# Gated feed-forward: the rounding of x with the grid offset made by a maximum inside VectorE's sums, and the subtraction moved to VectorE

## The chip, the cores and the metric

The kernel runs on one core of a Trainium2 chip. The metric is the device time of one execution in microseconds (us); of several runs the median is taken. The engines are named as in the profile: PE is TensorE (PEld its weight loads), DVE is VectorE, ACT is ScalarE, POOL is GpSimd, SP is SyncE.

## The reference

Six sub-blocks work on x, of shape (2, 2048, 256): twice a feed-forward with two routed experts and a shared one around a linear attention, then twice a gated feed-forward around a softmax attention. The change touches only the gated feed-forward, `_L1_ffn_ref`. Each of its three matrix products rounds both operands to a 4-bit grid with one scale for each block of 16 values:

```python
def fp4_quant_dequant(x):
    xb = x.reshape(shape[:-1] + (shape[-1] // BLOCK, BLOCK))      # BLOCK = 16
    scale = jnp.max(jnp.abs(xb), axis=-1, keepdims=True) / 6.0
    scale = jnp.maximum(scale, jnp.float32(1e-12))
    xn = xb / scale
    idx = jnp.searchsorted(_MID, jnp.abs(xn))
    q = _GRID[idx] * jnp.sign(xn) * scale        # 0, 0.5, 1, 1.5, 2, 3, 4, 6
    return q.reshape(shape)
...
gate = fp4_linear(x, w_gate)                     # 256 -> 704
y = fp4_linear(x, w_up)                          # 256 -> 704
h = jax.nn.silu(gate) * y
return fp4_linear(h, w_down)                     # 704 -> 256
...
x = x + 0.5 * _L1_ffn_ref(_layernorm(x, axis=-1), L1_ffn_w_gate, L1_ffn_w_up, L1_ffn_w_down)
```

## The kernel before

`build_program` writes six stages one after the other: `ffn0("a")`, `attn0()`, `ffn0("b")`, `ffn1("a", False)`, `attn1()`, `ffn1("b", True)`. The two calls of `ffn1` are the gated feed-forward, called the first and the second pass here. The order on each engine is written by hand, and every wait is on a semaphore.

The 4096 rows of x are 32 tiles of 128 rows (`T` = 32), which stay in SBUF. The weights were rounded to the grid in an earlier stage. A tile t goes through `ffn1` like this. ScalarE normalises it (L1684, tile `fxn`). The rounding of x, called x below (tiles `fxb`, `fxy`, `fxq`; 256 columns), runs three tiles ahead of the products (`AHEAD` = 3). TensorE transposes the rounded tile (L1591), ScalarE copies it out as a high part (L1691), TensorE subtracts that in PSUM (L1598), and ScalarE copies the rest, the low part (L1695). TensorE makes the gate and the up product from both parts (L1606, L1611). ScalarE applies Silu to the gate (L1718), VectorE multiplies by the up product in PSUM (L1774, tile `fh`, 704 columns). The rounding of h (tiles `fqb`, `fqy`, `fhq`; 704 columns) is done in the next turn of the loop. Three turns after its products (`LAG` = 3) TensorE transposes h (L1620, L1627, L1628), ScalarE copies its high part (L1723) and low part (L1732), and TensorE makes the down product (L1636 from the high part, L1642 from the low part, which waits for L1732). VectorE adds it to x (L1742), and in the first pass it also makes the statistics of the row for the next stage (L120, L122). The second pass (`store`) writes x out instead.

The rounding, class `QuantiseFour`, is the same for x and h. With s the scale of a block and y = v/s, adding c = max(1.5, |y|) x `STEP` to y rounds y in the float's last bits, and subtracting c again leaves the grid value. The steps are:

- step 0, L155: the largest absolute value of each block of 16, on VectorE; steps 1 and 2, L157 and L159: s and 1/s, on VectorE, on 16 columns for x and 44 for h
- step 3, L193: y, on VectorE; then |y| on ScalarE, L205
- step 4, L197: c = max(|y|, 1.5) x `STEP`, on VectorE, with one input tensor
- step 5, L201: r = y + c, on VectorE
- L175: r - c on GpSimd; L177: times s, on GpSimd

`order(t)` alternates the six steps of x of tile t + 3 with the six of h of tile t - 1 on VectorE; L1774 stands behind the eighth of the twelve, that is between step 3 and step 4. At the head of each turn stands L1742 of tile t - 4. In each turn GpSimd does L175 and L177 of h and then L175 and L177 of x. Before the loop VectorE rounds the x of tiles 0, 1 and 2 without anything between them, and GpSimd does their two operations, and between these it makes the low parts of the three weight matrices (L1798).

Of the kernel before, what the change touches and what calls it, by code (L numbers as in the profile page):

```python
# [11 lines left out]
ALU = mybir.AluOpType  # L12
ACT = mybir.ActivationFunctionType
AX = mybir.AxisListType

P = 128
# [6 lines left out]
BELOW = 1.0 - 2.0 ** -24  # L23
EXPONENT = 0x7F800000
MAGIC = 1.5 * 2.0 ** 22
STEP = 2.0 ** 22 - 4.0


class Event:
# [28 lines left out]
def build_program(nc, A):  # L58
    x_in = A["L0_attn_x"]
    nb, L, D = x_in.shape  # L60
# [19 lines left out]
    with ExitStack() as ctx:  # L80
        known = {}

        def event(name, by=1):
            if name not in known:
                known[name] = Event(ctx.enter_context(nc.semaphore(name)), by)
            return known[name]

        def sb(name, shape, dt=F32, scope=ctx):
            return scope.enter_context(nc.sbuf_tensor(name, shape, dt))

        def ring(scope, name, shape, n, dt=F32):
            return [sb(f"{name}{i}", shape, dt, scope) for i in range(n)]
# [17 lines left out]
        dv = Chain(ctx.enter_context(nc.semaphore("vector_own")))  # L110
# [24 lines left out]
        def blocks(ap):  # L135
            return ap.rearrange("p (k j) -> p k j", j=QB)

        class Quantise:
# [12 lines left out]
            def vector(self, e, step):  # L151
                if step > 0:
                    e.wait_ge(*self.at)
                if step == 0:
                    made = e.tensor_reduce(self.amax, blocks(self.src), AX.X, ALU.max, apply_absolute_value=True)  # L155
                if step == 1:
                    made = e.tensor_scalar(self.s, self.amax, INV_MAX, SCALE_FLOOR, ALU.mult, ALU.max)  # L157
                if step == 2:
                    made = e.reciprocal(self.rs, self.s)  # L159
                if step == 3:  # L160
                    made = e.scalar_tensor_tensor(out=blocks(self.y), in0=blocks(self.src), scalar=BELOW,
                                                  in1=self.spread(self.rs), op0=ALU.mult, op1=ALU.mult)
                if step == 4:
                    made = e.tensor_scalar(self.c.bitcast(I32), self.y.bitcast(I32), EXPONENT, None,
                                           ALU.bitwise_and)
                if step == 5:
                    made = e.tensor_scalar(self.c, self.c, 1.0, MAGIC, ALU.max, ALU.mult)
                if step == 6:
                    e.tensor_tensor(self.r, self.y, self.c, ALU.add).then_inc(*self.summed.up)
                    return  # L170
                made.then_inc(*dv.up())
                self.at = dv.now()

            def gpsimd(self, e):
                e.tensor_tensor(self.r, self.r, self.c, ALU.subtract).then_inc(*pl.up())  # L175
                e.wait_ge(*pl.now())
                e.tensor_tensor(blocks(self.out), blocks(self.r), self.spread(self.s),  # L177
                                ALU.mult).then_inc(*self.done.up)

        class QuantiseFour(Quantise):  # L180
# [3 lines left out]
            def events(self, n, scaled, magnitude):  # L184
                self.number, self.scaled, self.magnitude = n, scaled, magnitude
                return self

            def vector(self, e, step):
# [6 lines left out]
                if step == 4:  # L195
                    e.wait_ge(*self.magnitude(self.number + 1))
                    e.tensor_scalar(self.c, self.c, 1.5, STEP, ALU.max, ALU.mult).then_inc(*dv.up())  # L197
                    self.at = dv.now()
# [4 lines left out]
            def scalar(self, e):  # L203
                e.wait_ge(*self.scaled(self.number + 1))
                e.activation(self.c, self.y, ACT.Abs).then_inc(*self.magnitude.up)  # L205

        def constants():
            with nc.Block() as block:

                @block.vector  # L210
                def _(e):
                    e.memset(eps[:], LN_EPS).then_inc(*eps_ok.up)

                @block.gpsimd
                def _(e):
                    e.memset(wdT[R1:P, C1 - 1, :], 0.0).then_inc(*pl.up())
                    e.wait_ge(*pl.now())
                    e.memset(ident[:], 0.0).then_inc(*pl.up())
                    e.wait_ge(*pl.now())
                    e.affine_select(out=ident[:], in_=ident[:], compare_op=ALU.not_equal, fill=1.0, base=0,  # L220
                                    pattern=[[-1, P]], channel_multiplier=1).then_inc(*ident_ok.up)

                @block.sync
                def _(e):
                    e.dma_start(x[:, 0:GT, :], xin[:, 0:GT, :]).then_inc(*x_in_ok[0].up)

                @block.tensor
                def _(e):
                    e.wait_ge(*ident_ok(1))

                @block.scalar
                def _(e):
                    e.wait_ge(*eps_ok(1))
# [1304 lines left out]
        def ffn1(tag, store):  # L1538
            with ExitStack() as scope:
                W1 = C1 * P  # L1540
                XN, XQ = ring(scope, f"fxn{tag}", [P, D], 2), ring(scope, f"fxq{tag}", [P, D], 4)
# [5 lines left out]
                TMX = [(sb(f"fxb{tag}{i}", [P, 3, D // QB], scope=scope), sb(f"fxy{tag}{i}", [P, 3, D], scope=scope))  # L1547
                       for i in range(2)]
# [10 lines left out]
                xn_ok, xsum, xq_ok, xturn, xhi = (event(f"f1_{n}") for n in ("xn", "xsum", "xq", "xturn", "xhi"))  # L1559
# [4 lines left out]
                xy, xabs, hy, habs = (event(f"f1_{n}") for n in ("xy", "xabs", "hy", "habs"))  # L1564
# [3 lines left out]
                    return ap.rearrange("p (j n) -> p j n", j=2)  # L1568

                def quantise_x(t):  # L1570
                    return QuantiseFour(XN[t % 2][:], D, P, TMX[t % 2], XQ[t % 4][:], xsum, xq_ok).events(t, xy, xabs)

                def quantise_h(t):
                    return QuantiseFour(HB[t % 2][:], H1, P, TMH[t % 2], HQ[t % 3][:, 0:H1], hsum, hq_ok).events(t, hy, habs)
# [7 lines left out]
                with nc.Block() as block:  # L1582
# [97 lines left out]
                    def _(e):  # L1680
# [20 lines left out]
                        normal(0)  # L1701
                        normal(1)
                        quantise_x(0).scalar(e)
                        normal(2)
                        quantise_x(1).scalar(e)
                        e.activation(wu[0][:], wuT[:], ACT.Copy).then_inc(*whi_ok.up)
                        normal(3)
                        quantise_x(2).scalar(e)
                        e.activation(wd[0][:], wdT[:], ACT.Copy).then_inc(*whi_ok.up)
                        high_x(0)  # L1710
# [561 lines left out]
```

## Time and profile before

| what | value |
|---|---|
| median of 3 runs | 3412.04 us (3410.95 to 3433.1) |
| the profiled execution | 3422.33 us, its span 3420.3 us |
| busy over the span | PE 3212.1 us (94%), DVE 2529.7 (74%), ACT 2023.8 (59%), POOL 736.3 (22%) |
| first pass, about 1205 to 1500 us | PE 256.22 of 295, DVE 261.73, ACT 151.37, POOL 157.65 |
| second pass, about 3146 to 3420 us | PE 246.36 of 274, DVE 241.86, ACT 148.83, POOL 172.87 |

The profile is of one execution, which took 10 us more than the median, so a step is costed against its own span, and the difference is then set against the median. A timeline row gives the start from the span's beginning and the duration, both in us, then engine, line, operation, output<-inputs and shapes; in brackets stands the idle time of the engine before it and what ended that. An operation that had to wait for a port after it was started shows the wait in its duration and not in brackets. Numbers of double buffers are left out of names, and the last letter of a name, a or b, is the pass.

### The profile page before, as it was taken

Reading aid. Unit: us, or ns where it says so; the run is one execution under the profiler, and the core shown is the slowest. Engines: PE = TensorE matmul, PEld = TensorE weight load, DVE = VectorE, ACT = ScalarE, POOL = GpSimd, SP = SyncE. Lnnn points to the kernel's source line nnn. Section 1 sums busy time; section 2 is a strip of 40 time slices with the busy share of each in tenths; the row PEclk is TensorE's granted clock in tenths of the full one; section 3 lists DMA queues with packets and bytes.
Section 4 is the critical chain, followed back from the end, with each engine's and each line's share of the span. In section 5 each row is a group of like instructions: output and inputs, shape, how many; then the busy total and the mean of one; then the engine's idle time right before and its main releaser. Section 6 shows DMA issues by size and latency. Waiting matters only on the chain. (4 is left out here: it accounts for less than half of the span.)

```text
span 3420.3 us, 54248 instructions
## 1 busy us (share of the span) xinstructions
PE 3212.1 (94%) x20420; PEld 2117.2 (62%) x20420; DVE 2529.7 (74%) x4826; ACT 2023.8 (59%) x3764; POOL 736.3 (22%) x740
## 2 busy tenths in 40 slices
PE   7999979997999979988999999999999999997999
PEld 6899967776899969963444333344333333332998
DVE  7433658766433689948888888998888999972997
ACT  5544534335544545542777777777677777765554
POOL 3322334443322355520000000000000000001665
PEclk9999989999999989996999989999989999987999
DMA  3210210002211200023003030302003030000000
GB/s 127 79 44 32 62 45 1 1 2 78 73 44 38 62 1 1 1 76 49 14 26 50 2 39 2 39 1 31 9 2 38 2 39 2 2 2 0 13 14 25
DMA packets 60930, 99.91 MB, mean 29 GB/s; under 512 B 7632, under 2 KB 44160, under 8 KB 57984
## 3 DMA queue, kind: packets, MB, share of 16 engines
q1 hardware_dynamic: 54144, 78.62, 10.5%
q0 software_dynamic: 6528, 17.83, 1.6%
q8 instruction: 164, 2.69, 0.3%
q14 instruction: 94, 0.77, 0.1%
HBM read 65.36 MB, written 30.93 MB: 28 GB/s over the span
## 5 line engine op out<-in xcount | busy, mean ns | idle before, releaser
L2186 DVE TENSOR_REDUCE smxp<-psum 128x1 f32<-128x512 f32 x2048 | 1277.3, 683 | 159.0 <-PE psum L2051 144.9
L2146 ACT ACTIVATE spr<-psum 128x512 f32<-128x512 f32 x2048 | 1082.5, 599 | 453.6 <-PE psum L2070 445.5
L2070 PE MATMUL psum<-sqs,sks 50*128 50x512 f32 x2048 | 754.7, 470 | 5.4 <-ACT spr L2146 2.8
L2051 PE MATMUL psum<-sks,sqs 48*128 48x512 f32 x2048 | 678.4, 458 | 13.2 <-DMA sqs<-q_parts 12.8
L2051 PEld LDWEIGHTS psum<-sks,sqs 48*128 48x128 f32 x2048 | 292.7, 199 | 523.3 <-issue 462.0
L2084 PE MATMUL psum<-spr,sv 128*32 128x512 f32 x4096 | 576.9, 636 | 1.8 <-ACT spr L2146 0.7
L2070 PEld LDWEIGHTS psum<-sqs,sks 50*128 50x128 f32 x2048 | 323.3, 194 | 199.0 <-ACT spr L2146 167.9
L1801 POOL MEMSET fhqb<- 128x64 f32 x3 | 0.3, 152 | 1651.5 <-POOLq L1964 1651.5
L490 PE MATMUL psum<-w_a,hsa_hi 128*128 128x256 f32 (+1 forms) x1088 | 198.4, 281 | 0.1
L490 PE MATMUL psum<-w_b,hsb_hi 128*128 128x256 f32 (+1 forms) x1088 | 197.2, 280 | 0.4 <-DVE hsb_lo L740 0.4
L490 PEld LDWEIGHTS psum<-w_a,hsa_hi 128*128 128x128 f32 x1088 | 176.2, 189 | 12.6 <-DVE hsa_lo L740 1.2
L740 DVE TENSOR_TENSOR hsb_lo<-hidb,hsb_hi 128x512 fp32r<-128x512 f32 x136 | 94.3, 694 | 120.9 <-ACT hidb L585 120.3
L490 PEld LDWEIGHTS psum<-w_b,hsb_hi 128*128 128x128 f32 x1088 | 175.4, 188 | 12.3 <-DVE hsb_lo L740 0.9
L740 DVE TENSOR_TENSOR hsa_lo<-hida,hsa_hi 128x512 fp32r<-128x512 f32 x136 | 95.5, 703 | 116.4 <-ACT hida L585 115.7
L2084 PEld LDWEIGHTS psum<-spr,sv 128*32 128x32 f32 x4096 | 83.0, 110 | 152.3 <-issue 125.2
L490 PE MATMUL psum<-w_a,hsa_lo 128*128 128x256 f32 (+1 forms) x544 | 152.4, 280 | 0.0
L490 PE MATMUL psum<-w_b,hsb_lo 128*128 128x256 f32 (+1 forms) x544 | 151.9, 279 | 0.0
L473 PE MATMUL psum<-xTa_hi,w_a 128*128 128x512 f32 x288 | 106.8, 413 | 4.9 <-DVE xTa_lo L729 3.5
L473 PE MATMUL psum<-xTb_hi,w_b 128*128 128x512 f32 x288 | 104.9, 406 | 3.3 <-DVE xTb_lo L729 1.9
L490 PEld LDWEIGHTS psum<-w_a,hsa_lo 128*128 128x128 f32 x544 | 102.9, 189 | 0.0
L490 PEld LDWEIGHTS psum<-w_b,hsb_lo 128*128 128x128 f32 x544 | 102.4, 188 | 0.0
L584 ACT ACTIVATE hsa_hi<-psum,bwa 128x512 fp32r<-128x512 f32 x64 | 44.1, 689 | 97.4 <-issue 83.6
(417 smaller groups left out, 6149.8 us busy)
## 6 DMA issues: line engine op xcount, KB each, us to landing
sks<-q_parts SPq DMA_DIRECT2D x42, 256.0 KB, 9.4
sqs<-q_parts SPq DMA_DIRECT2D x42, 256.0 KB, 19.8
q_parts<-spart SPq DMA_DIRECT2D x16, 512.0 KB, 3.0
f_routed_a<-yoa SPq DMA_DIRECT2D x9, 512.0 KB, 2.9
f_routed_b<-yob SPq DMA_DIRECT2D x9, 512.0 KB, 2.9
x<-in_L_attn_x_dram SPq DMA_DIRECT2D x8, 512.0 KB, 7.3
yoa<-in_L_ffn_w_dram SPq DMA_DIRECT2D x16, 256.0 KB, 2.6
xga<-f_sorted_a SPq DMA_DIRECT2D x8, 512.0 KB, 3.8
```

The lines of the kernel that those rows point to most:

```text
L473: m = e.matmul(psum[:, n % 3, :], w[u][:, k, :], XT[p % 2][v][:, k, :], start=(k == j == 0), stop=(k == KD - 1 and j == 2))
L490: m = e.matmul(ops[:, i // 2, (i % 2) * D:(i % 2 + 1) * D], hs[u][:, i * P:(i + 1) * P], w2[:, v, ex, c, :], start=(c == 0 and i % 2 == 0 ...
L584: e.activation(hi[:], psum[:, n % 3, :], ACT.Relu, bias=bias)
L740: e.tensor_tensor(lo[:], HB[n % 2][:], hi[:].bitcast(F32), ALU.subtract).then_inc(*low_ok.up)
L1801: m = e.memset(hq[:, H1:], 0.0)
L2051: e.matmul(bank(what), QS[n % 2][rows, pr, q0:q0 + P], KS[n % 2][rows, pr, jc * GW:(jc + 1) * GW], start=True, stop=True, tile_position=(H ...
L2070: e.matmul(st[s % 3], KS[n % 2][rows, pr, jt * P:(jt + 1) * P], QS[n % 2][rows, pr, ic * GW:(ic + 1) * GW], start=True, stop=True, tile_po ...
L2084: m = e.matmul(po[32 * hq:32 * hq + VW, :], VB[b][:, jt, c0:c0 + VW], PR[j % 2][:, hq, :], start=(jt == 0), stop=(jt == TB - 1), tile_posi ...
L2146: e.activation(PR[j % 2][:, hq, :], st[s % 3], ACT.Exp, scale=float(DH) ** -0.5).then_inc(*exp_ok.up)
L2186: e.tensor_reduce(out[:, r // (2 * GT * IC), r // (2 * IC) % GT, r // 2 % IC, r % 2:r % 2 + 1], bank(what), AX.X, ALU.max).then_inc(*pm_fr ...
```

## The change

For x, class `QuantiseFour` is replaced by a new class, `QuantiseMax`; h stays as it was. Step 3 makes -y; ScalarE makes |y| x `STEP` through the scale of the activation. Step 4 takes the maximum with `LEAST` = 1.5 x `STEP`, which is c, and adds -y to it in one instruction, so that c is never written. Step 5 makes the same maximum again and subtracts what step 4 left from it, which gives the rounded y. GpSimd only multiplies by s.

```diff
+LEAST = 1.5 * STEP
...
+        class QuantiseMax(Quantise):
...
+            def vector(self, e, step):
+                if step < 3:
+                    super().vector(e, step)
+                if step == 3:
+                    e.wait_ge(*self.at)
+                    e.scalar_tensor_tensor(out=blocks(self.y), in0=blocks(self.src), scalar=-BELOW,
+                                           in1=self.spread(self.rs), op0=ALU.mult, op1=ALU.mult).then_inc(*self.scaled.up)
+                if step == 4:
+                    e.wait_ge(*self.magnitude(self.number + 1))
+                    e.scalar_tensor_tensor(out=self.r, in0=self.c, scalar=LEAST, in1=self.y, op0=ALU.max,
+                                           op1=ALU.add).then_inc(*dv.up())
+                    self.at = dv.now()
+                if step == 5:
+                    e.wait_ge(*self.at)
+                    e.scalar_tensor_tensor(out=self.r, in0=self.c, scalar=LEAST, in1=self.r, op0=ALU.max,
+                                           op1=ALU.subtract).then_inc(*self.summed.up)
+
+            def scalar(self, e):
+                e.wait_ge(*self.scaled(self.number + 1))
+                e.activation(self.c, self.y, ACT.Abs, scale=STEP).then_inc(*self.magnitude.up)
+
+            def gpsimd(self, e):
+                e.tensor_tensor(blocks(self.out), blocks(self.r), self.spread(self.s),
+                                ALU.mult).then_inc(*self.done.up)
...
                 def quantise_x(t):
-                    return QuantiseFour(XN[t % 2][:], D, P, TMX[t % 2], XQ[t % 4][:], xsum, xq_ok).events(t, xy, xabs)
+                    return QuantiseMax(XN[t % 2][:], D, P, TMX[t % 2], XQ[t % 4][:], xsum, xq_ok).events(t, xy, xabs)
```

The two places at which the prediction looks are these. On VectorE (DVE), from step 3 of x in one turn of the loop in the first pass (tiles of x: `fxya`, of h: `fqya`), before and then after:

```order
L193 SCALAR_TENSOR_TENSOR fxya<-fxna,fxba 128x256
L193 SCALAR_TENSOR_TENSOR fqya<-fha,fqba 128x704
L1774 TENSOR_TENSOR fha<-psum,fsga 128x704
L197 TENSOR_SCALAR fxya<-fxya 128x256
L197 TENSOR_SCALAR fqya<-fqya 128x704
L201 TENSOR_TENSOR fxya<-fxya 128x256
L201 TENSOR_TENSOR fqya<-fqya 128x704
L1742 SCALAR_TENSOR_TENSOR x<-psum,x 128x256
```

```order
L223 SCALAR_TENSOR_TENSOR fxya<-fxna,fxba 128x256
L194 SCALAR_TENSOR_TENSOR fqya<-fha,fqba 128x704
L1810 TENSOR_TENSOR fha<-psum,fsga 128x704
L227 SCALAR_TENSOR_TENSOR fxya<-fxya 128x256
L198 TENSOR_SCALAR fqya<-fqya 128x704
L232 SCALAR_TENSOR_TENSOR fxya<-fxya 128x256
L202 TENSOR_TENSOR fqya<-fqya 128x704
L1778 SCALAR_TENSOR_TENSOR x<-psum,x 128x256
```

Nothing moves there; two instructions of x have another form (L227 for L197, L232 for L201), and the line numbers are higher. On GpSimd (POOL), the start of the second pass up to the first rounding of h (`fqyb`, `fhqb`), before and then after:

```order
L1798 TENSOR_TENSOR fwg_lob<-wgT,fwg_hib 128x1408
L175 TENSOR_TENSOR fxyb<-fxyb 128x256
L177 TENSOR_TENSOR fxqb<-fxyb,fxbb 128x256
L175 TENSOR_TENSOR fxyb<-fxyb 128x256
L177 TENSOR_TENSOR fxqb<-fxyb,fxbb 128x256
L1798 TENSOR_TENSOR fwu_lob<-wuT,fwu_hib 128x1408
L175 TENSOR_TENSOR fxyb<-fxyb 128x256
L177 TENSOR_TENSOR fxqb<-fxyb,fxbb 128x256
L1798 TENSOR_TENSOR fwd_lob<-wdT,fwd_hib 128x1536
L175 TENSOR_TENSOR fxyb<-fxyb 128x256
L177 TENSOR_TENSOR fxqb<-fxyb,fxbb 128x256
L175 TENSOR_TENSOR fqyb<-fqyb 128x704
```

```order
L1834 TENSOR_TENSOR fwg_lob<-wgT,fwg_hib 128x1408
L240 TENSOR_TENSOR fxqb<-fxyb,fxbb 128x256 x2
L1834 TENSOR_TENSOR fwu_lob<-wuT,fwu_hib 128x1408
L240 TENSOR_TENSOR fxqb<-fxyb,fxbb 128x256
L1834 TENSOR_TENSOR fwd_lob<-wdT,fwd_hib 128x1536
L240 TENSOR_TENSOR fxqb<-fxyb,fxbb 128x256
L176 TENSOR_TENSOR fqyb<-fqyb 128x704
L178 TENSOR_TENSOR fhqb<-fqyb,fqbb 128x704
```

The subtractions of x (L175 on `fxyb`) are gone there, 32 in each pass, and the multiplies (L240, before L177) follow one another or the work on h.

## Rows read from the trace of the kernel before

**Rows 1.** Windows view, busy us per engine (x instructions), clock: steady stretches of both passes.

```profile
1262.00:1479.00 217.00, 208.55 (x1437) 199.05 (x1437) 204.89 (x418) 116.52 (x208) 121.59 (x106) 1.00 0.00 1
...
3193.00:3405.00 212.00, 211.07 (x1498) 205.25 (x1497) 200.88 (x379) 120.22 (x216) 143.34 (x110) 1.00 0.06 19
```

**Rows 2.** DVE timeline, L1742 at either end of 25 tiles, then one.

```profile
1254.07 0.42 DVE L1742 SCALAR_TENSOR_TENSOR x<-psum,x 128x256 f32<-128x256 f32 x1
...
1455.68 0.42 DVE L1742 SCALAR_TENSOR_TENSOR x<-psum,x 128x256 f32<-128x256 f32 x1 [0.29 <-PE psum L1642]
...
3192.78 0.43 DVE L1742 SCALAR_TENSOR_TENSOR x<-psum,x 128x256 f32<-128x256 f32 x1
...
3380.38 0.42 DVE L1742 SCALAR_TENSOR_TENSOR x<-psum,x 128x256 f32<-128x256 f32 x1 [0.28 <-PE psum L1642]
...
3387.68 0.42 DVE L1742 SCALAR_TENSOR_TENSOR x<-psum,x 128x256 f32<-128x256 f32 x1 [0.17 <-PE psum L1642]
```

**Rows 3.** DVE timeline, one tile of the first pass (start us, us).

```profile
1353.03 0.86 DVE L157 TENSOR_SCALAR fxba<-fxba 128x16 f32<-128x16 f32 x1
...
1354.39 0.48 DVE L193 SCALAR_TENSOR_TENSOR fxya<-fxna,fxba 128x256 f32<-128x256 f32 x1
1354.79 1.30 DVE L193 SCALAR_TENSOR_TENSOR fqya<-fha,fqba 128x704 f32<-128x704 f32 x1
...
1357.79 0.88 DVE L201 TENSOR_TENSOR fqya<-fqya 128x704 f32<-128x704 f32 x1
```

**Rows 4.** POOL timeline, the same tile of the first pass.

```profile
1352.48 1.39 POOL L177 TENSOR_TENSOR fhqa<-fqya,fqba 128x704 f32<-128x704 f32 x1
1353.83 0.76 POOL L175 TENSOR_TENSOR fxya<-fxya 128x256 f32<-128x256 f32 x1
1354.66 0.68 POOL L177 TENSOR_TENSOR fxqa<-fxya,fxba 128x256 f32<-128x256 f32 x1
```

**Rows 5.** PE timeline, the same tile: idle time before it in brackets.

```profile
1357.94 0.98 PE L1642 MATMUL psum<-fwd_hia,fhTa_lo 128*128 128x256 f32 x6 [0.31 <-ACT fhTa_lo L1732]
```

**Rows 6.** DVE timeline, one tile of the second pass.

```profile
3267.88 0.42 DVE L1742 SCALAR_TENSOR_TENSOR x<-psum,x 128x256 f32<-128x256 f32 x1 [0.27 <-PE psum L1642]
...
3269.34 0.17 DVE L157 TENSOR_SCALAR fxbb<-fxbb 128x16 f32<-128x16 f32 x1
...
3270.03 1.15 DVE L193 SCALAR_TENSOR_TENSOR fxyb<-fxnb,fxbb 128x256 f32<-128x256 f32 x1
3271.10 1.42 DVE L193 SCALAR_TENSOR_TENSOR fqyb<-fhb,fqbb 128x704 f32<-128x704 f32 x1
```

**Rows 7.** POOL timeline, the same tile of the second pass.

```profile
3267.69 1.72 POOL L175 TENSOR_TENSOR fqyb<-fqyb 128x704 f32<-128x704 f32 x1 [2.17 <-DVE fqyb L201]
3269.48 1.42 POOL L177 TENSOR_TENSOR fhqb<-fqyb,fqbb 128x704 f32<-128x704 f32 x1
3270.86 0.92 POOL L175 TENSOR_TENSOR fxyb<-fxyb 128x256 f32<-128x256 f32 x1
3271.86 1.15 POOL L177 TENSOR_TENSOR fxqb<-fxyb,fxbb 128x256 f32<-128x256 f32 x1
```

**Rows 8.** Source views, durations ns min/median/max: DVE forms of 256 columns.

```profile
L193 DVE SCALAR_TENSOR_TENSOR fxya<-fxna,fxba x32: 363/480/1223, 1214.8 to 1451.1; 128x256 f32<-128x256 f32 x32
...
L197 DVE TENSOR_SCALAR fxya<-fxya x32: 276/278/2726, 1215.7 to 1453.5; 128x256 f32<-128x256 f32 x32
...
L201 DVE TENSOR_TENSOR fxya<-fxya x32: 409/414/426, 1216.0 to 1454.2; 128x256 f32<-128x256 f32 x32
...
L789 DVE SCALAR_TENSOR_TENSOR x<-yoa,x x32: 403/418/426, 382.6 to 426.5; 128x256 f32<-128x256 f32 x32
```

**Rows 9.** DVE timeline, second x tile before the first pass's loop.

```profile
1216.84 0.47 DVE L157 TENSOR_SCALAR fxba<-fxba 128x16 f32<-128x16 f32 x1
...
1217.63 0.63 DVE L193 SCALAR_TENSOR_TENSOR fxya<-fxna,fxba 128x256 f32<-128x256 f32 x1
```

**Rows 10.** POOL timeline, the same stretch.

```profile
1217.36 0.62 POOL L177 TENSOR_TENSOR fxqa<-fxya,fxba 128x256 f32<-128x256 f32 x1
```

More of the change, by code:

```diff
@@ L205, in scalar, with events @@
                 e.activation(self.c, self.y, ACT.Abs).then_inc(*self.magnitude.up)
+        class QuantiseMax(Quantise):
+            def events(self, n, scaled, magnitude):
+                self.number, self.scaled, self.magnitude = n, scaled, magnitude
+                return self
+            def vector(self, e, step):
[20 more added lines that the diff above has]
+                                ALU.mult).then_inc(*self.done.up)
         def constants():
```

## The prediction

> **What bounds the kernel now.** I read the busy time by stage first, since the change touches only the two gated feed-forward passes (the fourth and the last of the six stages). In their steady stretches TensorE is busy 96% and over 99% of the time and VectorE 94% and 95% [rows 1], so the shares don't say which of them sets the pace. The spacing of the residual add L1742, one per tile, does better: from 1254.07 to 1455.68 there are 25 tiles, 8.06 us each, in the first pass, and from 3192.78 to 3380.38 again 25, 7.50 each, in the second [rows 2]. The tile after that, without an x to quantise, takes 7.30 us with TensorE at work throughout. So some 7.3 us is what TensorE needs, and there are 0.8 us a tile above it in the first pass, 0.2 in the second.
>
> I call the instructions by line, with x or h for what they quantise: L177h is GpSimd's multiply of h. The timelines of VectorE and GpSimd laid side by side show where the 0.8 us go. L157x is an operation on 16 columns and takes 0.86 us: it ends at 1353.89, when L177h on GpSimd has just ended (1353.87). L193x ends at 1354.87, 0.28 after L175x (1354.59); L193h ends at 1356.09, 0.75 after L177x (1355.34) [rows 3, 4]. The second pass shows the same and the reverse: L193x ends 0.28 after L177h; L175x, which started at 3270.86, ends 0.60 after L193x; L193h ends 0.74 after L175x; and L177x, which takes 0.62 alone [rows 10], ends 0.49 after L193h, having taken 1.15 [rows 6, 7]. The two engines take turns: GpSimd's operations exclude VectorE's two-input ones (256 columns cost 0.27 of such time, 704 columns 0.74) and the other way round. I call what they take turns at the port. The reduction and the product from PSUM at L1774 aren't held.
>
> **The loop that sets the period** is then one through both engines. In the first pass, with T the end of L177h (1353.87): L193h ends at T+2.22, L201h at T+4.80 (1358.67), and the next L177h at T+8.06. Nothing in it waits except for the port. The other loop, L193h to ScalarE to TensorE's L1642 to L1742 and back, has slack: L1642 starts 1.85 after L193h ends, waiting 0.31 for ScalarE, and is done at 1358.92 [rows 5], 2.83 after it; L1742 and what follows reach L157x some 0.84 us before the port is free. In the second pass no statistics follow L1742, VectorE asks for the port earlier in GpSimd's cycle, L157x slips through between L175h and L177h, and it is L193x that waits (1.15 us) until L177h is done.
>
> **The change, part by part.** *Form of the scaling and of Abs:* a sign and a factor, same shapes, nothing. *First sum:* a tensor_scalar of 256 columns, 0.278, becomes a scalar_tensor_tensor with two inputs. The same form in place elsewhere, L789, takes 0.418; the difference is +0.14 [rows 8]. *Subtraction:* the tensor_tensor of 0.414 becomes a scalar_tensor_tensor of 0.418, +0.00 [rows 8]. Both lie behind L1774, when GpSimd has finished with the tile's work, so no port wait is added; but they are on the loop, between L193h and L201h, so the 0.14 counts in full. *GpSimd:* the subtraction L175x goes, and the multiply L177x follows L177h at once.
>
> First pass: L157x ends at T+0.02 as before, L193x starts at T+0.52. The multiply starts at T-0.04 and takes 0.62 [rows 10], a little more for the hold by VectorE's small operations, so it is over at T+0.58 to T+0.62. L193x alone takes 0.36 [rows 8], of which the last 0.27 need the port: it would take it at T+0.61, and hardly waits. It ends at T+0.88, not T+1.00; L193h starts 0.08 before that and takes 0.88, as L201h does [rows 3], with nothing to wait for: T+1.68, not T+2.22. That is -0.54 for the waits and +0.14 for the sum, **-0.40 a tile**, 7.66 us. Covers: TensorE needs 7.3, so L1774, which waits for the tile's second product, finds it ready at this pace; L1742 could start 0.15 after L201h instead of 0.29, and L157x would still come 0.98 before T. So the same loop stays the bound, and 25 tiles give -10.0 us.
>
> Second pass: L193x still waits for L177h and ends 0.28 after it. Then the multiply (0.49 of port time) stands where the subtraction did (0.60), and L193h waits for it, -0.11 or -0.10. With +0.14 the tile gets longer by 0.03, 7.53 us; 25 tiles give +0.8, and the three without L1742 at the start of each pass, which show this second pattern too, +0.2. The bounds of a tile here are +0.14, if the multiply holds the port as long as the subtraction, and -0.2, where TensorE's 7.3 stops any gain.
>
> Before the loop, in both passes, tiles 0 to 2 are quantised one after the other, and L157x (0.47) and L193x (0.63, ending 0.28 after L177x) are held by GpSimd for tiles 1 and 2 [rows 9, 10]. Without the subtraction I put them at 0.35 and 0.42, -0.33 a tile, against +0.14 each for tiles 0 and 1: -0.4 us until ScalarE may write the first transposed x, which TensorE waits for. Bounds: 0 and -0.9, the length of one subtraction with its handover. Twice -0.4 is -0.8.
>
> **Sum:** -10.0 + 0.8 + 0.2 - 0.8 = -9.8 us. The profiled execution took 3422.3 us (span 3420.3) and would take 3412.5; the median of the timed runs lies 10 us lower, at 3412.0, and as no row ties that difference to the feed-forward, I take the same -9.8 off it: **3402 us**.
>
> **A page against a row.** The row: one two-input operation and one GpSimd operation never overlap in their port time [rows 6, 7]. The Trainium skill, SBUF — State Buffer, on the shared port pair, has it as an exclusive lock, held for a whole instruction, taken by whoever starts first; the trace agrees on the exclusion. If both engines shared the port's rate instead, the relief would be half as large, some -5 us. The Trainium skill, Perfetto Trace Analysis, Optimizing Scalar/DVE Operations, says for the same reason that moving operations between GpSimd and VectorE "might not help"; and that a saturated VectorE may give work away, which is the reverse of this change.
>
> **Rivals.** *The multiply takes the subtraction's place in the first pass too, slower (0.17).* The place is L193x at T+0.6. If the multiply isn't quite over there and L193x goes first, the multiply resumes behind it, and L193h waits again: T+2.12, -0.10 + 0.14 = +0.04 a tile. Both passes then lose, 50 tiles by 0.04 and the first ones 0.2, less 0.8: 3413.4; with a multiply of 0.60 port time, +0.14 a tile, 3418. It decides at some 0.03 us, which the rows can't exclude; against it speaks that an operation under way isn't interrupted in any row. "Might not help", in the Trainium skill's words quoted above, would be borne out here.
>
> *The gap is missed in the second pass (0.12).* L1742 comes closer to L201h by 0.14, so L157x asks before L175h ends; if the pair of small operations L157 falls behind L177h instead, the second pass takes the first's pattern, 7.67 us a tile, +0.17 and not +0.03: 3402 + 25 x 0.14 = 3405.5. Against: L157x needs the port for under 0.1 us, and 0.08 lie between L175h and L177h.
>
> *TensorE becomes the bound (0.08).* If the port waits go altogether in the first pass and L193h's chain allows it, the tile falls to 7.3: 25 x 0.76 = 19 us, 3393. VectorE would allow it: of the 8.06, port waits are 1.23 (0.69 in L157x, which takes 0.17 alone [rows 6], 0.12 and 0.42 in the two L193) and the wait before L1742 0.29, so its own work with the 0.14 more is 6.7. Against it stands the loop through GpSimd, worked out above.
>
> **How the numbers follow.** Forecast 0.58 (3399 to 3405), the slower rival 0.17, the missed gap 0.12, TensorE 0.08, 0.05 for what I don't see. The range takes 3395 to 3414: forecast, missed gap and most of the slower rival. A difference within 1%, 34 us, is about what a measurement of this kernel can't tell from none (the three runs spread over 22 us). No case reaches it: faster 0.02, same 0.96, slower 0.02, for the unseen and a bad run.
>
> **What would show it.** L1742 spaced by 7.66 in the first pass and 7.53 in the second; L193x at 0.36 to 0.40 and L193h at 0.88 in the first pass, 1.15 and 1.3 in the second; both new forms at 0.41 to 0.42; L157x still at 0.86 in the first pass; L1642's wait in the first pass shrinking; the first matmul of the loop 0.4 earlier. A period of 8.1 with L193h at 1.2 or more is the slower rival; 7.3 with no wait before L1642 is TensorE. I would be wrong by more than the range if the new form were slower than L789's, or if the engines fell into a third pattern of turns.

## The result

The changed kernel took 3409.1 us (median of 22 runs, 3391.5 to 3463.8), the kernel before on the same chips 3428.6 us (22 runs, 3406.4 to 3463.6). The ratio is 0.9946, with a 95% interval of 0.9924 to 0.9968: faster by half a per cent, within the 1% that was called no change. The chip has a second, slower state, and the ratios, like the line through runs of the kernel before that is drawn further down, leave out the runs that fell in it (3 of the 22 of the changed kernel), so a ratio isn't quite the quotient of two medians. The profiled execution took 3425.1 us, its span was 3423.4, longer than that of before, so the whole says little, and the two passes have to be read by themselves. In the timelines the ends of 25 tiles are, as in [rows 2] (L1778 is L1742 of before):

```profile
1269.28 0.42 DVE L1778 SCALAR_TENSOR_TENSOR x<-psum,x 128x256 f32<-128x256 f32 x1
...
1460.62 0.42 DVE L1778 SCALAR_TENSOR_TENSOR x<-psum,x 128x256 f32<-128x256 f32 x1
...
3196.91 0.42 DVE L1778 SCALAR_TENSOR_TENSOR x<-psum,x 128x256 f32<-128x256 f32 x1
...
3383.68 0.42 DVE L1778 SCALAR_TENSOR_TENSOR x<-psum,x 128x256 f32<-128x256 f32 x1
```

The first pass now makes a tile in 191.34/25 = 7.65 us, for 8.06, the second in 186.77/25 = 7.47, for 7.50. With the start and the end of each pass, from the offsets of the normalisation to the last residual add, worked out in the same way from each timeline ("the rest" is from the last of these tiles to the last residual add of the pass):

| us | before | after |
|---|---|---|
| first pass: start to first residual add / 25 tiles / the rest | 43.8 / 201.6 / 36.5 | 44.0 / 191.3 / 36.6 |
| second pass: the same | 43.9 / 187.6 / 36.1 | 44.4 / 186.8 / 35.9 |
| both passes | 549.5 | 539.0 |
| span's start to the first pass | 1210.3 | 1225.2 |
| first pass to second | 1656.7 | 1655.4 |

The passes got 10.5 us shorter. The stages ahead of the first pass, which the change doesn't touch, took 15 us longer in this execution.

One tile of the first pass on VectorE, which answers to [rows 3] (L158 was L157, L223 and L194 were L193 of x and of h, L227 and L232 were L197 and L201 of x, L202 was L201 of h):

```profile
1345.90 0.42 DVE L1778 SCALAR_TENSOR_TENSOR x<-psum,x 128x256 f32<-128x256 f32 x1
...
1348.02 1.02 DVE L158 TENSOR_SCALAR fxba<-fxba 128x16 f32<-128x16 f32 x1
...
1349.54 0.36 DVE L223 SCALAR_TENSOR_TENSOR fxya<-fxna,fxba 128x256 f32<-128x256 f32 x1
1349.82 0.88 DVE L194 SCALAR_TENSOR_TENSOR fqya<-fha,fqba 128x704 f32<-128x704 f32 x1
...
1351.42 0.41 DVE L227 SCALAR_TENSOR_TENSOR fxya<-fxya 128x256 f32<-128x256 f32 x1
...
1352.19 0.41 DVE L232 SCALAR_TENSOR_TENSOR fxya<-fxya 128x256 f32<-128x256 f32 x1
1352.53 0.88 DVE L202 TENSOR_TENSOR fqya<-fqya 128x704 f32<-128x704 f32 x1
```

and the same tile on GpSimd, which answers to [rows 4] (L176, L178 and L240 were L175h, L177h and L177x):

```profile
1345.83 1.71 POOL L176 TENSOR_TENSOR fqya<-fqya 128x704 f32<-128x704 f32 x1 [3.87 <-DVE fqya L202]
1347.62 1.39 POOL L178 TENSOR_TENSOR fhqa<-fqya,fqba 128x704 f32<-128x704 f32 x1
1348.97 0.64 POOL L240 TENSOR_TENSOR fxqa<-fxya,fxba 128x256 f32<-128x256 f32 x1
```

With T the end of the multiply of h (1349.01): L158x waits for it still, 1.02 us, and ends at T+0.03. The multiply of x ends at T+0.60, L223 starts at T+0.53 and takes 0.36, the scaling of h (L194) takes 0.88 and ends at T+1.69. Both port waits behind the first one are gone. In the second pass, for [rows 6, 7], VectorE first and then GpSimd:

```profile
3265.61 0.22 DVE L158 TENSOR_SCALAR fxbb<-fxbb 128x16 f32<-128x16 f32 x1
...
3266.32 1.23 DVE L223 SCALAR_TENSOR_TENSOR fxyb<-fxnb,fxbb 128x256 f32<-128x256 f32 x1
3267.47 1.31 DVE L194 SCALAR_TENSOR_TENSOR fqyb<-fhb,fqbb 128x704 f32<-128x704 f32 x1
```

```profile
3264.09 1.71 POOL L176 TENSOR_TENSOR fqyb<-fqyb 128x704 f32<-128x704 f32 x1 [3.55 <-DVE fqyb L202]
3265.88 1.39 POOL L178 TENSOR_TENSOR fhqb<-fqyb,fqbb 128x704 f32<-128x704 f32 x1
3267.23 0.80 POOL L240 TENSOR_TENSOR fxqb<-fxyb,fxbb 128x256 f32<-128x256 f32 x1
```

Here L223 still waits (1.23 us), ending 0.28 after the multiply of h (3267.27); the multiply of x ends 0.48 after that, and L194 0.75 later again. The order of turns is that of before with the subtraction left out. The two new forms in the source views, for [rows 8], minimum, median and maximum in ns:

```profile
L227 DVE SCALAR_TENSOR_TENSOR fxya<-fxya x32: 406/409/425, 1230.7 to 1458.5; 128x256 f32<-128x256 f32 x32
...
L232 DVE SCALAR_TENSOR_TENSOR fxya<-fxya x32: 408/412/426, 1231.1 to 1459.3; 128x256 f32<-128x256 f32 x32
```

### The profile page after: what moved, and what is told of

Read it like the earlier page. It is cut to its first block and busy times, and to the rows that moved or that the text cites. A ratio compares the mean times of both kernels' runs of the same rounds, so it can differ in the third digit from the quotient of the medians.

```text
span 3423.4 us, 54184 instructions
## 1 busy us (share of the span) xinstructions
PE 3202.7 (94%) x20420; PEld 2108.2 (62%) x20420; DVE 2526.5 (74%) x4826; ACT 2022.9 (59%) x3764; POOL 671.4 (20%) x676
## 3 DMA queue, kind: packets, MB, share of 16 engines
q1 hardware_dynamic: 54144, 78.62, 10.5%
## 5 line engine op out<-in xcount | busy, mean ns | idle before, releaser
L620 ACT ACTIVATE hsa_hi<-psum,b_a 128x512 fp32r<-128x512 f32 x72 | 49.5, 688 | 98.1 <-issue 67.2
L620 ACT ACTIVATE hsb_hi<-psum,b_b 128x512 fp32r<-128x512 f32 x72 | 49.6, 688 | 96.9 <-issue 70.2
```

The lines of the kernel that those rows point to most:

```text
L620: e.activation(hi[:], psum[:, n % 3, :], ACT.Relu, bias=bias)
```

## The experiments

All passes below are measured as in the table above. For reference, before: 8.06 and 7.50 us a tile; after: 7.65 and 7.47.

**The form alone.** The kernel before, with L197 of x as a two-input instruction; `grid` is a constant tile filled with `STEP`.

```diff
-    e.tensor_scalar(self.c, self.c, 1.5, STEP, ALU.max, ALU.mult).then_inc(*dv.up())
+    e.scalar_tensor_tensor(out=self.c, in0=self.c, scalar=1.5, in1=self.grid, op0=ALU.max,
+                           op1=ALU.mult).then_inc(*dv.up())
```

> The kernel before with one instruction of x in another form: the tensor_scalar of step 4 (L197, 0.278 us) is a scalar_tensor_tensor with a second input, a constant tile of STEP. GpSimd keeps subtraction and multiply. Theory, the period is a loop through VectorE and GpSimd with no slack: the 0.14 us count in full in every tile, 8.20 us in the first pass and 7.64 in the second, +7 us in all, ratio to before 1.002. Rival, there is slack on VectorE (it waits 0.28 us before the residual add, and TensorE needs about 7.3 us a tile): the periods stay at 8.06 and 7.50.

Measured: ratio 1.0012 (0.9972 to 1.0051), which tells nothing; the trace does. The 25 tiles take 8.20 and 7.60 us each, +0.14 and +0.09, and both passes together 555.5 us, +6.0, of which the 50 tiles are 5.8. (The starts got 1.3 and 1.4 us shorter and the end of the first pass 2.8 longer, which nearly cancels. TensorE's granted clock goes with it: from 30 to 40 us after the reciprocal with which the first pass begins it was 0.91 and 0.75, for 0.76 and 0.55 before, and at its end it fell to 0.50 for 5 us, where it was 1.00 before.) So VectorE's 0.28 us of waiting before L1742 were no slack, and 0.14 us on an instruction that nobody waits for directly arrive at the end nearly in full. In the first pass that is as expected. In the second it is 0.05 less: start to start the new form takes 0.13 us more than L197 did, and GpSimd's multiply of h takes 1.39 us there instead of 1.42 [rows 7].

**The subtraction as an instruction of its own.** The kernel before; steps 4 and 5 of x as they were, GpSimd only multiplies, and in the loop the new step stands ahead of the last sum of h.

```diff
+                if step == 6:
+                    e.wait_ge(*self.at)
+                    e.tensor_tensor(self.r, self.r, self.c, ALU.subtract).then_inc(*self.summed.up)
...
-                e.tensor_tensor(self.r, self.r, self.c, ALU.subtract).then_inc(*pl.up())
-                e.wait_ge(*pl.now())
```

> The kernel before with the subtraction of x on VectorE as a tensor_tensor of its own, behind the sum; GpSimd only multiplies; the forms of steps 4 and 5 stay. Theory, the waits for the port go as in the changed kernel (-0.54 us in the first pass, -0.10 to -0.17 in the second) and 0.34 us of VectorE come onto the loop: 7.86 us a tile in the first pass, 7.67 to 7.74 in the second, together about 0. Rival, the gain of the changed kernel comes from less work or from the new form of the sums, not from the waits: then 0.34 more on VectorE with the waits unchanged, 8.4 and 7.84.

Measured: ratio 1.0029 (0.9998 to 1.0061); tiles of 7.98 and 7.81 us (7.86 and 7.67 to 7.74 expected), both passes 559.3, +9.8, of which 5.4 are in the 50 tiles and 4.7 at the two starts (the next experiment says why; the scaling of tile 2 takes 3.13 us here). The port waits went as in the changed kernel: L193 takes 0.36 for x and 0.88 for h in the first pass. What was off is the new step's price, 0.45 and not 0.34. The sum, the subtraction and the sum of h on VectorE:

```profile
1355.78 0.41 DVE L214 TENSOR_TENSOR fxya<-fxya 128x256 f32<-128x256 f32 x1
1356.23 0.43 DVE L218 TENSOR_TENSOR fxya<-fxya 128x256 f32<-128x256 f32 x1
1356.57 0.89 DVE L201 TENSOR_TENSOR fqya<-fqya 128x704 f32<-128x704 f32 x1
```

The subtraction needs the sum just ahead of it and starts 0.45 us after it; the sum of h, which needs neither, starts 0.34 after the subtraction. With 0.45 the loop comes to 1.68 + 2.58 + 0.45 + 3.26 = 7.97, 7.98 measured. The rival (8.4 and 7.84) falls by the first pass; the period of the second, 7.81, wouldn't tell the two apart. The experiment also separates the change's two halves: leaving GpSimd's subtraction out is worth 0.54 us a tile in the first pass and 0.15 in the second (7.504 + 0.45 - 7.807), and what the maximum inside the sums does is to have the subtraction at 0.13 instead of 0.45.

**The weights' low parts later.** The changed kernel, with this order on GpSimd:

```diff
                         end_x(1)
-                        low_weights(1, wu, wuT)
                         end_x(2)
-                        low_weights(2, wd, wdT)
+                        low_weights(1, wu, wuT)
...
                                 end_x(t + AHEAD)
+                            if t == 0:
+                                low_weights(2, wd, wdT)
```

> The changed kernel with two of the weights' low parts later on GpSimd: that of the up weights behind x of tile 2 instead of ahead of it, that of the down weights behind x of tile 3, in the loop. Theory, the gain before the loop was lost because the low part of the up weights now starts just ahead of tile 2's scaling (3.06 us instead of 0.43): ScalarE writes the first transposed x 2.5 us earlier after the start of the pass, and the first residual add comes 1.5 to 2.5 us sooner, 3 to 5 us for both passes; steady periods stay at 7.65 and 7.47. Rival, the start is bound by something else (TensorE at half clock, the scalings' waits move to tile 3): the first residual add stays within 0.5 us.

It was made because the start of the passes had not got shorter by 0.4 but longer by 0.3 and 0.5. The rows say why. In the kernel before, tile 2's scaling on VectorE, the low part of the up weights on GpSimd, and TensorE's first correction:

```profile
1220.65 0.62 DVE L193 SCALAR_TENSOR_TENSOR fxya<-fxna,fxba 128x256 f32<-128x256 f32 x1
```

```profile
1220.95 3.38 POOL L1798 TENSOR_TENSOR fwu_loa<-wuT,fwu_hia 128x1408 fp32r<-128x1408 f32 x1
```

```profile
1223.42 0.58 PE L1598 MATMUL psum<-fxTa_hi,fnia 128*128 128x256 f32 x1 [4.64 <-ACT fxTa_hi L1691]
```

In the changed kernel, the scalings of tiles 1, 2 and 3, then GpSimd and TensorE:

```profile
1232.61 0.43 DVE L223 SCALAR_TENSOR_TENSOR fxya<-fxna,fxba 128x256 f32<-128x256 f32 x1
...
1235.45 3.06 DVE L223 SCALAR_TENSOR_TENSOR fxya<-fxna,fxba 128x256 f32<-128x256 f32 x1
...
1240.93 3.41 DVE L223 SCALAR_TENSOR_TENSOR fxya<-fxna,fxba 128x256 f32<-128x256 f32 x1
```

```profile
1234.48 0.62 POOL L240 TENSOR_TENSOR fxqa<-fxya,fxba 128x256 f32<-128x256 f32 x1 [2.22 <-DVE fxya L232]
1235.06 3.17 POOL L1834 TENSOR_TENSOR fwu_loa<-wuT,fwu_hia 128x1408 fp32r<-128x1408 f32 x1
```

```profile
1240.66 0.58 PE L1634 MATMUL psum<-fxTa_hi,fnia 128*128 128x256 f32 x1 [7.59 <-ACT fxTa_hi L1727]
```

In tile 1 the scaling L223 is free (0.43). In tile 2 it takes 3.06: GpSimd, done with x of tile 1 sooner by a subtraction, began the low part of the up weights at 1235.06, just ahead of it, and holds the port for 3.17 us. Before, that operation started after this scaling and met the next instruction, L197. Now ScalarE's |y| of tile 2 waits too, and behind it its copy of the down weights and of the first transposed x, and TensorE waits 7.59 us instead of 4.64: ScalarE writes the first transposed x 15.39 us after the reciprocal with which the pass begins, for 13.08 before. Tile 3 has the same with the down weights, 3.41.

Measured: the ratio is 0.9940 (0.9905 to 0.9975), the passes take 536.7 us, 2.3 less than after. The periods stay at 7.65 and 7.47, and ScalarE writes the first transposed x 12.66 us after the reciprocal and not 15.39, both as expected. Of this 2.7 the first residual add kept 2.0 in the second pass (42.3 for 44.4), in the first only 0.3 (43.7 for 44.0), which is where the rival put it, and the 2.3 in all fall short of the 3 to 5 expected. The windows of the two passes of this kernel, 30 to 35 and 35 to 40 us after that reciprocal in each (the third number from the end is the granted clock):

```profile
1252.29:1257.29 5.00, 1.96 (x10) 1.70 (x9) 5.00 (x8) 2.35 (x5) 1.80 (x2) 0.78 0.01 2
1257.29:1262.29 5.00, 5.00 (x21) 4.93 (x20) 5.00 (x9) 1.64 (x3) 3.85 (x3) 0.54 0.00 0
3176.36:3181.36 5.00, 3.55 (x22) 3.29 (x21) 5.00 (x8) 2.63 (x6) 1.67 (x2) 0.96 0.01 3
3181.36:3186.36 5.00, 5.00 (x38) 4.91 (x37) 5.00 (x10) 1.98 (x4) 3.85 (x3) 1.00 0.00 0
```

In the first pass TensorE ran at 0.78 and then 0.54 of its clock, near the lower of its two levels, 1.2 of 2.4 GHz, in the second at 0.96 and 1.00 (it had 0.70 there from 25 to 30). It had idled 3.04 us ahead of tile 3's correction (L1634) in the first pass and 1.45 in the second, so the same edit lands on either side. The stall by the port is shown; what a start costs in the end goes with a clock that differs between these runs, and what moved the clock is not shown.

**The new form for h.** The changed kernel, with `QuantiseMax` for h as well:

```diff
-                    return QuantiseFour(HB[t % 2][:], H1, P, TMH[t % 2], HQ[t % 3][:, 0:H1], hsum, hq_ok).events(t, hy, habs)
+                    return QuantiseMax(HB[t % 2][:], H1, P, TMH[t % 2], HQ[t % 3][:, 0:H1], hsum, hq_ok).events(t, hy, habs)
```

> The changed kernel with the new form for h too: step 4 of h is a two-input instruction (0.88 us for 0.51, +0.36 on VectorE), the subtraction of h (1.71 us) leaves GpSimd. Theory, the loop through both engines is the bound of the changed kernel: without the 1.78 us between the last sum of h and GpSimd's multiply it is about 7.0 us long in the first pass and shorter in the second, so TensorE's own 7.3 us becomes the period in both: -0.35 and -0.17 us a tile, -13 us for 50 tiles against the changed kernel, ratio to before 0.993. Rival, VectorE's own sum of work is the bound (6.7 us of work and what it waits): then +0.36 a tile, 8.0 and 7.8.

Measured: ratio 0.9876 (0.9839 to 0.9913), 7.30 and 7.31 us a tile, 521.7 us for both passes, 27.8 below before. The 50 tiles are 13.0 below the changed kernel, as expected; the starts and ends are 4.3 below it too, and the ratio lies below the 0.993 expected. One tile of the first pass on VectorE, then GpSimd (L240 is the multiply, of h and of x):

```profile
1351.84 0.89 DVE L232 SCALAR_TENSOR_TENSOR fqya<-fqya 128x704 f32<-128x704 f32 x1
1352.65 0.42 DVE L1778 SCALAR_TENSOR_TENSOR x<-psum,x 128x256 f32<-128x256 f32 x1
...
1354.77 0.17 DVE L158 TENSOR_SCALAR fxba<-fxba 128x16 f32<-128x16 f32 x1
...
1355.45 0.36 DVE L223 SCALAR_TENSOR_TENSOR fxya<-fxna,fxba 128x256 f32<-128x256 f32 x1
1355.73 0.88 DVE L223 SCALAR_TENSOR_TENSOR fqya<-fha,fqba 128x704 f32<-128x704 f32 x1
1356.87 0.89 DVE L1810 TENSOR_TENSOR fha<-psum,fsga 128x704 f32<-128x704 f32 x1 [0.26 <-PE psum L1647]
```

```profile
1352.81 1.40 POOL L240 TENSOR_TENSOR fhqa<-fqya,fqba 128x704 f32<-128x704 f32 x1 [5.33 <-DVE fqya L232]
1354.16 0.62 POOL L240 TENSOR_TENSOR fxqa<-fxya,fxba 128x256 f32<-128x256 f32 x1
```

No port wait is left in this pass: L158x takes 0.17, L223 0.36 and 0.88. GpSimd is through with both multiplies at 1354.78, as L158x asks for the port (1354.77). VectorE waits for TensorE's product in nearly every tile (0.26 in brackets, L1810), and in the windows view TensorE is busy for all of the 170 us from 1280 to 1450. In the second pass one port wait is left (the small operation L158 of h, 0.60 for 0.18), and VectorE's wait for TensorE, 0.51 there, covers it. The rival, VectorE's work as the bound, falls.

**Both, and h alone.** Three more: the new form for x and h with the weights later; the form for h alone (x in `QuantiseFour` again); the latter with the weights later. The edit of the second against the kernel before; in the others the edits shown above are added:

```diff
                 def quantise_x(t):
                     return QuantiseFour(XN[t % 2][:], D, P, TMX[t % 2], XQ[t % 4][:], xsum, xq_ok).events(t, xy, xabs)
...
                 def quantise_h(t):
-                    return QuantiseFour(HB[t % 2][:], H1, P, TMH[t % 2], HQ[t % 3][:, 0:H1], hsum, hq_ok).events(t, hy, habs)
+                    return QuantiseMax(HB[t % 2][:], H1, P, TMH[t % 2], HQ[t % 3][:, 0:H1], hsum, hq_ok).events(t, hy, habs)
```

> The same with the two low parts of the weights later, as in the run before of that kind: 1 to 3 us below the run with the new form for h and x, from before the first residual add alone; periods 7.3 in both passes.

Measured: ratio 0.9891 (0.9855 to 0.9927), 7.30 us a tile, both passes 517.9 us, 3.8 below the run with the form for h and x (1 to 3 expected); the first residual add comes at 41.0 and 40.8 us instead of 43.6 and 42.1 in the run with the form for h and x.

> The new form for h alone, x as in the kernel before (tensor_scalar, and subtraction and multiply on GpSimd). Theory, of GpSimd's operations only those of h lie on the loop ahead of VectorE's requests; without the subtraction of h those of x fall before step 3 asks, mostly: TensorE's 7.3 us is the period in both passes here too, and the new form for x adds nothing to that for h (difference under 0.1 us a tile). Rival, each subtraction on GpSimd costs VectorE its own wait: then this is slower than the form for both, by the 0.5 us that it gave x in the first pass.

Measured: ratio 0.9907 (0.9874 to 0.9940), 7.32 and 7.30 us a tile, both passes 519.0 us. VectorE and GpSimd in the first pass:

```profile
1354.64 0.16 DVE L158 TENSOR_SCALAR fxba<-fxba 128x16 f32<-128x16 f32 x1
...
1355.33 0.42 DVE L194 SCALAR_TENSOR_TENSOR fxya<-fxna,fxba 128x256 f32<-128x256 f32 x1
1355.67 0.88 DVE L223 SCALAR_TENSOR_TENSOR fqya<-fha,fqba 128x704 f32<-128x704 f32 x1
```

```profile
1352.68 1.39 POOL L240 TENSOR_TENSOR fhqa<-fqya,fqba 128x704 f32<-128x704 f32 x1 [4.51 <-DVE fqya L232]
1354.03 0.73 POOL L176 TENSOR_TENSOR fxya<-fxya 128x256 f32<-128x256 f32 x1
1354.84 0.62 POOL L178 TENSOR_TENSOR fxqa<-fxya,fxba 128x256 f32<-128x256 f32 x1
```

The subtraction of x is back on GpSimd, 0.73 us from 1354.03, and costs VectorE 0.06 us in the first pass (0.42 for 0.36): it lies where VectorE asks for nothing. In the second pass it does make VectorE wait. L158 of h takes 0.72 for the 0.60 with both forms, and the scaling of x 0.56 for 0.36:

```profile
3270.35 0.72 DVE L158 TENSOR_SCALAR fqbb<-fqbb 128x44 f32<-128x44 f32 x1
...
3271.44 0.56 DVE L194 SCALAR_TENSOR_TENSOR fxyb<-fxnb,fxbb 128x256 f32<-128x256 f32 x1
```

The period is 7.30 all the same, because TensorE sets it: VectorE's wait for the product shrinks from 0.51 to 0.33. So the same subtraction that was worth 0.54 us behind the work of h is worth nothing without it, in the first pass by its place and in the second because TensorE's pace hides it. The theory's 7.3 holds, the rival's +0.5 doesn't.

> The new form for h alone, and the two low parts of the weights later on GpSimd. Before the loop x has its subtraction on GpSimd again, so that the low part of the up weights starts later: I expect the first residual add 0 to 2 us sooner than with the new form for h alone, periods of 7.3.

Measured: ratio 0.9894 (0.9857 to 0.9931), 7.32 and 7.31 us a tile, both passes 521.1 us; the first residual add at 42.3 and 42.2 us, where h alone had 40.3 and 42.2. The gain of 0 to 2 us at the start did not come; in the first pass it became a loss of 1.9, with the clock at 0.76 from 25 to 30 us after the reciprocal, where h alone had 1.00. The edit that gained 2.6 and 1.3 us with the form for x and h had nothing to gain here: ScalarE writes the first transposed x 13.03 us after the reciprocal, and with h alone it did so after 13.09. Why the clock differed is not shown.

**The changed kernel again.**

> The changed kernel once more, beside the kernel before on this chip. The traces of before and after give the two feed-forward passes 10.5 us less together, ratio 0.997. If the 0.9946 measured is more than these passes, another stage must be shorter as well: from the end of one pass to the start of the next, and from the start of the span to the first pass, in the same direction in this run too. If it is scatter, these stretches differ either way.

Measured: ratio 0.9961 (0.9923 to 1.0000), both passes 538.9 us (539.0 in the first trace), first residual adds at 43.8 and 44.4. The passes repeat within 0.2 us. The stretch between them doesn't: 1624.5 us against 1655.4 in the first trace of the same kernel. Two windows inside that stretch, of this run and of the last one above:

```profile
1510.00:3115.00 1605.00, 1539.98 (x8776) 626.19 (x8775) 1362.23 (x2339) 1135.29 (x2187) 0.00 (x0) 0.96 0.14 23
```

```profile
1500.00:3155.00 1655.00, 1591.26 (x8752) 642.61 (x8751) 1359.17 (x2332) 1135.61 (x2181) 0.00 (x0) 0.92 0.14 21
```

The granted clock is 0.96 in the one and 0.92 in the other. In the ten traces the stretch between the passes lies between 1624.5 us (0.96) and 1681.3 (0.92), and follows the clock; the stretch ahead of the first pass lies between 1210.3 (before) and 1231.5, for which no reason is shown. Scatter of 57 us in a stage that no edit touches is what the ratio has to be seen through.

## Why the prediction was right

The forecast was -9.8 us, 3402 us against 3412. The passes gave -10.5, and the ratio -0.54% (0.32 to 0.76), which is 11 to 26 us; the predicted 0.29% lies just outside that interval, and so does the 0.31% of the traces. That the 3409.1 us measured lie in the range of 3395 to 3414 is luck in part: the range was laid around the 3412.0 of three runs of the kernel before, and 22 runs of it give 3428.6, from which 9.8 less is 3418.8. The medians are 19.5 us apart, twice the forecast.

Other stages have no part in it that repeats: the second trace of the changed kernel has the stretch between the passes 31 us shorter than the first, and both traces of it start the first pass later than before.

Why the timed ratio lies a little below what the passes give, 0.9969, is answered in the main by the granted clock of the runs. For the runs of the kernel before that stand beside the experiments it is on record (49 runs, clocks of 0.944 to 0.968): a straight line through them falls by 2.45 us for each 0.001 of clock, and they scatter around it by 2.6 us. The changed kernel's runs lie 9.9 us below this line, with an error of 0.5, and those of the repetition 10.1; the passes say 10.5 and 10.7. The other seven kernels lie within 3 us of what their passes say: the form alone at +5.8 (6.0 by the passes), the subtraction alone at +7.9 (9.8), the new form for h and x at -29.2 (-27.8), that for h alone at -28.7 (-30.5). The rest of the measured difference goes with a mean clock of 0.960 against 0.957; whether the change or chance made it higher is open. So the timed runs and the traces agree on some 10 us.

- **The bound.** The prediction took the loop through VectorE, GpSimd and the port as the bound and TensorE's 7.3 us as the floor. Adding 0.13 us (the form alone) and 0.45 (the subtraction alone) on VectorE showed the loop, the new form for h showed the floor, 7.30 and 7.31.
- **First pass.** 7.66 us a tile forecast, 7.65 measured; the waits fell by 0.53 (T+1.69 for T+2.22) against 0.54, L194's wait as a whole and L223's. The sum's price was 0.13, with 0.14 forecast.
- **Second pass.** 7.53 forecast, 7.47 measured, 0.03 below before and not above: a term mis-sized. From T to the end of L194 it is 1.51 us, 1.62 before, the -0.11 that was expected. But the multiply of h ends 3.18 us after the subtraction of h starts, not 3.21 as in [rows 7], and from the end of L194 to that of L202 it is 2.70 for 2.59, so this stretch grew by 0.11 and not by 0.14, the difference of two durations: start to start the new form takes 0.33 where L197 took 0.20, +0.13, and the last 0.02 are within the rounding of the rows. The other 0.03 is the multiply of h itself, 1.39 us for 1.42, here and with the form alone. What held it before is not shown. Over 25 tiles that is -0.8 instead of +0.8.
- **The start of the passes.** This step was wrong: -0.4 us each forecast, +0.3 and +0.5 measured to the first residual add, and ScalarE's first transposed x came 2.3 us later (15.39 for 13.08) and not 0.4 sooner. It summed the two waits that go (in tile 1, 0.47 to 0.37 and 0.63 to 0.43, as expected) and looked at GpSimd's queue as far as x, not at the long operation queued behind it. That one moved from 0.30 us behind the start of tile 2's scaling to 0.39 ahead of it. The experiment on the weights shows it. That only 0.3 and 0.5 of the 2.3 reach the first residual add goes with TensorE's clock: from 30 to 40 us after the reciprocal it was 1.00 and 0.66 in the first pass, for 0.76 and 0.55 before, and 1.00 throughout in the second, for 0.78 and 0.53.
- **The sum's share.** -10.27 in the first pass's 25 tiles and -0.83 in the second's, +0.74 at the starts and -0.17 at the ends: -10.53. Two misses of opposite sign, +1.3 at the starts (forecast -0.8 and the 0.2 of the three tiles) and -1.6 in the second pass, nearly cancel; the forecast's agreement to 0.7 us is partly luck.
- **The rivals.** The multiply didn't take the subtraction's place in the first pass: it ended 0.60 after T, as worked out, and L223 needs the port from T+0.62. The gap was nearly missed in the second pass (L158x takes 0.22 instead of 0.17), at no price. TensorE wasn't the bound, with this change. A port whose rate the two engines share, for which the prediction gave some -5 us, doesn't fit either: the first pass alone gave -10.3.

**The version that beats both** is the new form for h, with or without that for x: 519 to 522 us for both passes against 539.0 and 549.5, ratios to before of 0.988 to 0.991; with x and h and the weights later 517.9. Which of these is the fastest the ratios don't tell.

## What to carry to other kernels

Where two engines take turns at a port, an operation costs what it delays at the other engine and not its own length: the same subtraction was worth 0.54 us, 0.15 or nothing, depending on what stood ahead of it and on whether TensorE set the pace. Lay both timelines side by side and look for operations whose duration grows while nothing is in brackets, and when GpSimd gets lighter, follow its whole queue to the next long operation, since that moves up too. Take out first the operation that stands between the last result and the next request, which here was that of h.

## What was not expected of the hardware

- A VectorE operation of 16 columns waited for GpSimd's multiply to end, as the big ones do: 1.02 us for L158x in the changed kernel, ending 0.03 behind the multiply, 0.16 without a wait.
- Start to start, a two-input operation of 256 columns took 0.34 us where the next one didn't need its result and 0.45 where it did (the sum and the subtraction in the second experiment).
- The clock that TensorE was granted in the softmax attention differed from run to run between 0.92 and 0.96, with up to 57 us between the shortest and the longest.
